# Linear attention's output projection made token-major, with the queries ahead of the values and a third exponential buffer

## What is computed

```
Q, K = phi(h @ Wq), phi(h @ Wk)          # phi(x) = elu(x) + 1; 16 heads of 64
V    = h @ Wv
S, z = cumsum(K (x) V), cumsum(K)        # over the tokens of a sequence
out  = (Q . S) / max(Q . z, 1e-6)        # per head, per token
x    = x + out @ Wo                      # Wo is 1024 x 128: the output projection
```

## Time and profile before

| what | value |
|---|---|
| median of 3 runs | 841.12 us (841.11 to 843.43) |
| profiled execution, its own time | 841.11 us |
| its span | 839.3 us |
| busy: PE, PEld | 790.7 us (94%), 669.6 us (80%) |
| busy: DVE, ACT, POOL | 558.6 us (67%), 571.5 us (68%), 354.2 us (42%) |
| chain that ended last, by engine | PE 68%, ACT 13%, DVE 9%, issue 4%, POOL 4% |
| granted TensorE clock, mean | 0.999 |

### The profile page before, as it was taken

How to read it: one execution, slowest core, us unless ns; L and a number is a source line. 1 busy time by engine, 2 the same in 40 slices (tenths; PEclk the granted TensorE clock), 3 DMA queues, 4 the chain that set the end, 5 groups by cost and what they waited for, 6 DMA issues and landing times.

```text
span 839.3 us, 27765 instructions
## 1 busy us (share of the span) xinstructions
PE 790.7 (94%) x11682; PEld 669.6 (80%) x11682; DVE 558.6 (67%) x1313; ACT 571.5 (68%) x1024; POOL 354.2 (42%) x284
## 2 busy tenths in 40 slices
PE   1799999999999999999999999999889999999997
PEld 0588878877788888888888888888777888888885
DVE  8665656454877877787877867876979682828220
ACT  3787878767646666556666566666578887878774
POOL 4597979774101001010010101000236597979784
PEclk9999999999999999999999999999999999999999
DMA  7001111111000101010010100201015220201010
GB/s 263 0 26 45 57 40 36 35 55 51 16 3 24 29 0 51 0 38 12 0 50 0 51 0 10 78 0 37 28 51 152 76 64 12 63 14 51 1 51 27
DMA packets 56700, 33.53 MB, mean 40 GB/s; under 512 B 1984, under 2 KB 55232, under 8 KB 56640
## 3 DMA queue, kind: packets, MB, share of 16 engines
q1 hardware_dynamic: 56640, 32.79, 13.5%
HBM read 22.29 MB, written 10.49 MB: 39 GB/s over the span
## 4 chain that ended last, share of the span: by engine, by line
PE 68%; ACT 13%; DVE 9%; issue 4%; POOL 4%; DMA 1%; SPq 0%; ACTq 0%; DVEq 0%; POOLq 0%
PE ps L690 33%; PE ps L864 15%; PE ps L661 6%; PE ps L927 4%; PE ps L938 3%; PE ps L758 3%; ACT rr L1236 3%; ACT ee L1235 3%; DVE ol L1662 3%; PE ps L954 2%; ACT vt L1257 2%; ACT kf L1265 2%; PE ps L910 2%; POOL alA L1780 1%; POOL alB L1780 1%
## 5 line engine op out<-in xcount | busy, mean ns | idle before, releaser
L1235 ACT ACTIVATE ee<-ps 128x512 f32<-128x512 f32 x128 | 77.9, 609 | 96.8 <-PE ps L864 62.7
L1880 POOL TENSOR_TENSOR as<-as,power 128x4 f32<-128x4 f32 x16 | 19.0, 1189 | 285.9 <-DVE as L1585 255.7
L1403 DVE SCALAR_TENSOR_TENSOR full<-ps,sc,gate 128x512 f32<-128x512 f32 x64 | 46.6, 748 | 105.8 <-PE ps L690 63.3
L1780 POOL TENSOR_TENSOR alA<-full,ahA 128x512 fp32r<-128x512 f32 x74 | 100.6, 1372 | 35.6 <-DVE ahA L1411 29.5
L690 PE MATMUL ps<-ahA,wh 128*128 128x512 f32 x288 | 113.7, 395 | 1.3 <-POOL alA L1780 1.3
L690 PE MATMUL ps<-ahB,wh 128*128 128x512 f32 x288 | 113.4, 394 | 0.6 <-POOL alB L1780 0.6
L690 PE MATMUL ps<-alA,wh 128*128 128x512 f32 x288 | 112.3, 390 | 0.0
L690 PE MATMUL ps<-alB,wh 128*128 128x512 f32 x288 | 112.2, 390 | 0.0
L1780 POOL TENSOR_TENSOR alB<-full,ahB 128x512 fp32r<-128x512 f32 x76 | 99.5, 1322 | 13.3 <-ACT ahB L1136 7.4
L1135 ACT ACTIVATE full<-ps,sc 128x512 f32<-128x512 f32 x86 | 59.5, 691 | 33.5 <-PE ps L690 23.1
L1236 ACT ACTIVATE rr<-ps 128x512 f32<-128x512 f32 x128 | 78.2, 611 | 0.0
(11 more groups left out here) (181 smaller groups left out, 2178.3 us busy)
## 6 DMA issues: line engine op xcount, KB each, us to landing
wst<-in_ternary SPq DMA_DIRECT2D x5, 512.0 KB, 7.1
stage<-in_attn SPq DMA_DIRECT2D x4, 512.0 KB, 4.8
xlnA<-x_scratch SPq DMA_DIRECT2D x8, 256.0 KB, 2.8
axr<-x_scratch SPq DMA_DIRECT2D x8, 256.0 KB, 3.1
yx_scratch<-ay SPq DMA_DIRECT2D x8, 256.0 KB, 2.3
xs_scratch<-axs SPq DMA_DIRECT2D x8, 256.0 KB, 2.4
xlnA<-yx_scratch SPq DMA_DIRECT2D x8, 256.0 KB, 2.8
xlnB<-yx_scratch SPq DMA_DIRECT2D x8, 256.0 KB, 2.8
```

What stands on the lines that cost most here:

```text
L1235: nc.scalar.activation(ee[k][:, :], src[:, :], ACT.Exp).then_inc(*X["act"].step(f"e_{name}"))
L1403: nc.vector.scalar_tensor_tensor(fulll[m][:, :], ps[f["bank"]["L1", U, m, "v", n]][:, :], sc[:, KT + m:KT + m + 1], gate[k % NS][:, :], AL ...
L1780: return nc.gpsimd.tensor_tensor(dst, src, hi.bitcast(F32), ALU.subtract)
```

## The change

The operands of the output projection change places. The outputs `oh`, `ol` are stationary now, 128 tokens at a time, and Wo moves, 128 columns wide. The result has tokens on the partitions, so the copy to `ayf` and the two transposes go and DVE adds the residual straight from the projection's bank. The query groups are issued before the values on PE, on ACT and in the turns of the banks. A third pair of `ee`, `rr` buffers is added (`NE = 3`). The turn that belonged to the two transposes is still taken, by nothing.

```diff
-            NE = 2
-            ee = [sb(s, f"ee{k}", [P, TILE]) for k in range(NE)]
-            rr = [sb(s, f"rr{k}", [P, TILE]) for k in range(NE)]
+            NE = 3
+            ee = [sb(s, f"ee{k}", [P, TILE]) for k in range(NE - 1)]
+            rr = [sb(s, f"rr{k}", [P, TILE]) for k in range(NE - 1)]
...
-            ayf = sb(s, "ayf", [P, TILE // 2])
...
-            sb(s, "unused4", [P, PR, TILE // 2])
+            ee.append(sb(s, f"ee{NE - 1}", [P, TILE]))
+            rr.append(sb(s, f"rr{NE - 1}", [P, TILE]))
+            sb(s, "unused4", [P, 2, TILE])
...
-                    job(bank, f"WO{hh - 1}", "act", f"wf{hh - 1}")
-                    act.append(f"wf{hh - 1}")
+                    job(bank, f"WO{hh - 1}", "dve", f"y{hh - 1}")
+                    dve.append(f"y{hh - 1}")
...
-                bank = turn()
-                if hh:
-                    job(bank, f"yT{hh - 1}", "dve", f"y{hh - 1}")
-                    dve.append(f"y{hh - 1}")
+                turn()
...
-                for j, h in ((0, None), (1, None), (2, 0), (3, 1)):
+                for j in range(4):
                     phi(turn(), f"Q{hh + 1}.{j}")
-                    if h is not None:
-                        values(turn(), o + 1, h)
+                for h in range(2):
+                    values(turn(), o + 1, h)
...
             def output_projection(hh):
 
                 after("dve", f"ol{2 * hh + 1}.1")
-                three(bank(f"WO{hh}")[:, 0:2 * P],
-                      [(wah[:, 3 * DA + p * P:3 * DA + (p + 1) * P], wal[:, 3 * DA + p * P:3 * DA + (p + 1) * P],
-                        oh[:, p, :], ol[:, p, :]) for p in range(PR)], f"WO{hh}")
+                b = bank(f"WO{hh}")
+                for c in range(2):
+                    own = slice(c * P, (c + 1) * P)
+                    three(b[:, own], [(oh[:, p, own], ol[:, p, own], wah[:, 3 * DA + p * P:3 * DA + (p + 1) * P],
+                                       wal[:, 3 * DA + p * P:3 * DA + (p + 1) * P]) for p in range(PR)], f"WO{hh}" if c else None)
...
-                queries(hh + 1, 0)
-                queries(hh + 1, 1)
-                queries(hh + 1, 2)
-                token_major("V", o + 1, 0)
-                queries(hh + 1, 3)
-                token_major("V", o + 1, 1)
+                for j in range(4):
+                    queries(hh + 1, j)
+                for h in range(2):
+                    token_major("V", o + 1, h)
...
-            def output_rows(hh):
-                after("pe", f"WO{hh}")
...
-                nc.scalar.copy(ayf[:, :], ps[X["banks"].bank[f"WO{hh}"]][:, 0:2 * P]).then_inc(*X["act"].step(f"wf{hh}"))
...
             def residual(hh):
...
-                after("pe", f"yT{hh}")
+                after("pe", f"WO{hh}")
...
-                nc.vector.tensor_tensor(ay[:, own, :], ps[X["banks"].bank[f"yT{hh}"]][:, 0:2 * P].rearrange("p (q d) -> p q d", d=D),
+                nc.vector.tensor_tensor(ay[:, own, :], ps[X["banks"].bank[f"WO{hh}"]][:, 0:2 * P].rearrange("p (q d) -> p q d", d=D),
                                         axp[i % 2][:, own, :], ALU.add).then_inc(*X["dve"].step(f"y{hh}"))
```

More of the change, by code:

```diff
@@ L223, in build_kernel @@
             sb(s, "unused3", [P, 2, D])
-            NE = 2
-            ee = [sb(s, f"ee{k}", [P, TILE]) for k in range(NE)]
-            rr = [sb(s, f"rr{k}", [P, TILE]) for k in range(NE)]
+            NE = 3
+            ee = [sb(s, f"ee{k}", [P, TILE]) for k in range(NE - 1)]
+            rr = [sb(s, f"rr{k}", [P, TILE]) for k in range(NE - 1)]
             kf = sb(s, "kf", [P, PR, P])
             axr = sb(s, "axr", [P, Q, D])
-            ayf = sb(s, "ayf", [P, TILE // 2])
+            sb(s, "unused5", [P, TILE // 2])
             sb(s, "unused2", [P, TILE // 2])
@@ L478, in attention_plan @@
                     tail(1, "W0", "act_fy", "y", 0)
-                    job(2, f"WO{hh}", "act", f"wf{hh}")
-                    act.append(f"wf{hh}")
-                    job(7, f"yT{hh}", "dve", f"y{hh}")
+                    job(2, f"WO{hh}", "dve", f"y{hh}")
                     dve.append(f"y{hh}")
@@ L783, in f_last @@
                 elif t:
-                    after("act", f"wf{NHALF - 1}")
+                    after("dve", f"y{NHALF - 1}")
                 else:
@@ L810, in ffn_pe @@
                         tern_norm(0, "A", NI)
-                    if t == 2:
-                        back(NHALF - 1)
                     f_first(t, range(KT))
@@ L962, in transposed_outputs @@
                     transposes(bank(f"OT{g}.{j}"), [ot[:, 2 * p:2 * p + 2, :] for p in range(4 * j, 4 * j + 4)], X["pe"], f"OT{g}.{j}")
-            def back(hh):
-                after("act", f"wf{hh}")
-                transposes(bank(f"yT{hh}"), [ayf[:, q * P:(q + 1) * P] for q in range(2)], X["pe"], f"yT{hh}")
             def output_projection(hh):
                 after("dve", f"ol{2 * hh + 1}.1")
-                three(bank(f"WO{hh}")[:, 0:2 * P],
-                      [(wah[:, 3 * DA + p * P:3 * DA + (p + 1) * P], wal[:, 3 * DA + p * P:3 * DA + (p + 1) * P],
-                        oh[:, p, :], ol[:, p, :]) for p in range(PR)], f"WO{hh}")
+                b = bank(f"WO{hh}")
[3 more added lines that the diff above has]
+                                       wal[:, 3 * DA + p * P:3 * DA + (p + 1) * P]) for p in range(PR)], f"WO{hh}" if c else None)
             def attention_first():
@@ L999, in pair @@
                 transposed_keys(o)
-                if hh:
-                    back(hh - 1)
                 transposed_outputs(e)
@@ L1277, in outputs_high @@
                         .then_inc(*X["act"].step(f"oh{g}.{j}"))
-            def output_rows(hh):
-                after("pe", f"WO{hh}")
-                if hh:
-                    after("pe", f"yT{hh - 1}")
-                nc.scalar.copy(ayf[:, :], ps[X["banks"].bank[f"WO{hh}"]][:, 0:2 * P]).then_inc(*X["act"].step(f"wf{hh}"))
             def attention_first():
@@ L1308, in attention_act @@
                         f_norm(0)
-                    if hh:
-                        output_rows(hh - 1)
                     transposed_keys(o)
@@ L1320, in attention_act @@
                         f_evacuate(0)
-                        output_rows(hh)
                         continue
@@ L1324, in attention_act @@
                         exp_relu(f"K{o + 1}.{h}")
[L1325 to L1330, removed]
+                    for j in range(4):
+                        exp_relu(f"Q{hh + 1}.{j}")
+                    for h in range(2):
+                        values(o + 1, h)
                     transposed_keys(o + 1)
```

## The result

The changed kernel takes 872.52 us (median of 4 runs, 869.53 to 876.09) against 842.27 us for the kernel before in the same comparison (841.11 to 844.25): a ratio of 1.0357, 95% interval 1.0311 to 1.0404. The forecast was 874 us in a range of 846 to 884, with 0.90 on slower.

What follows compares the result with a forecast made beforehand. The prediction took PE to bound the attention halves. Its sum was 841.11 us + 38.7 for the projection - 6 for the third buffer and query order = 873.8, so 874 us, in a range of 846 to 884.

Steps and rivals of the forecast that it cites:

- The bound: In the attention stage's halves PE sets the time; without `once` a half would take about 27.2 us, with it 27.5.
- The product's price: Each of 48 projection products costs 115 ns by its weight load: 2.42 us more per half, 38.7 us over 16.
- The 81 ns of the Trainium skill: The skill's figure per 128-column matmul in a sustained stream; the projection would take 3.9 us, 0.8 us more per half.
- The copy and the residual: ACT's 16 dropped copies, 6.0 us, were costed at nothing; DVE's residual delays nobody, since `ol` still waits for ACT.
- Queries first, third buffer: PE gets about 0.85 us back in 7 halves with `once`, the order itself winning about 0: -6 us in all.
- The end of the stage: Near the last two projections PE also waits for DVE; up to 1.3 us could vanish there, left to the range.
- the clock: Sign of being wrong: a granted clock under 1.00 in the projection, PE moving columns only half the time.
- Rival 1: In the projection loads are hidden and columns set the price, 65 ns per product: 835.4 us, faster; chance 0.08.
- rival 2: In the projection loads are half hidden, 81 ns per product: 847.7 us; chance 0.05.
- rival 3: In the projection narrow fp32r products cost as plain f32, 244 ns each: 973 us; chance 0.09.
- Rival 4: For the queries, ACT's chain to `ol` stays as long and the -6 us become 0: 880 us; chance 0.10.

Runs made afterwards that it cites:

- e5: Changed kernel with each projection product loading 64 columns of weights instead of 128, same 128 moving columns, half the projection's rows left out: 833.09 us, single run.
- e6: Changed kernel with each projection product moving 64 columns of Wo instead of 128, same load, half the projection's columns left out: 913.63 us, single run.
- e9: e7 with high and low Wo side by side, so 32 products and loads per projection replace 48, and DVE adds twice: 845.88 us, ratio 1.0036.
- e1: Kernel before with the third buffer pair and the queries ahead of the values, old projection kept: 836.56 us, ratio 0.9925.
- e2: Changed kernel with two buffer pairs and the old order, so the new projection alone: 881.32 us, ratio 1.0427 against the kernel before.
- e10: Changed kernel run again unchanged; with its first set, 5 of 9 runs took 875.05 to 878.54 us, the others 869.53 to 870.43.
- e4: Kernel before with only the queries issued ahead of the values, on PE, ACT and in the banks' turns: 842.12 us, ratio 0.9999.
- e3: Kernel before with only the third buffer pair added: 837.68 us, ratio 0.9938.
- e7: Changed kernel with the last half's output projection issued on PE ahead of the transposes that wait for DVE: 869.35 us.
- e8: e1 with the last half's projection issued ahead of the transposes that wait for DVE: 836.08 us, ratio 0.9928 against the kernel before.

## Why the prediction was right, and where it was off

- **The bound.** Right. PE bounded the halves, and 2.21 us more on PE per projection gave 14.74 us first parts in place of 12.48. A half without `once` takes 27.11 us and one with it 27.10, for the 27.2 and 27.5 I had named.
- **The product's price.** I took 115 ns between the load's floor of 110 and the 120 ns of a 256-column product. It is 110.6: the floor itself. The term of the sum mis-sized is 38.7 us, which measured is 35.4, near the lower end I gave (34.9). e5 and e6 show the mechanism, that the load sets it, and e9 that the number of loads does.
- **The 81 ns of the Trainium skill** ("TensorE: Matmul & The Clock Gate", "Back-to-back issue gap"): no run agrees, 110.6 ns for a 128-column fp32r product. It was right not to let it set the sum. The same page of the Trainium skill, in "LDWEIGHTS (loading the stationary operand)", gives the time of a load in ns as its columns divided by 1.2, which is 107 for 128 and 53 for 64. The trace agrees for 128, at 110 ns between starts. For 64 it can't tell: e5's 60 ns may be the load's or that of the 128 moving columns, which I had put at 65 ns from the earlier trace rows.
- **The copy and the residual.** Right at nothing: ACT's idle time before `kf` took the copy's place, and `ol` still waits for ACT's `oh`, 45.5 us in all.
- **Queries first, third buffer.** The -6 us was right as a sum, in part by luck. The second parts of 15 halves add up to 6.1 us less than before, but what this part of the change gives is about 5: 4.9 us in e1 and 5.2 between e2 and the changed kernel, at full clock. In the trace 5.1 us come from six halves with `once`, 0.83 to 0.90 each, the price I had named. The seventh I had counted, the first half, is 0.7 us longer here and 0.15 in e10, and not shorter, and the second half, which I had at nothing, is 1.7 shorter, mostly by idle time of PE that is gone with the new projection (e2). The reading that the order wins nothing was right (e4), and so was the one that ACT's wait for `qf` was the thing to remove (e3). That Q3 would still meet a rest of the wait was right in two of these halves, with second parts of 12.53 and 12.50 us: there Q3 starts 0.70 and 0.66 us after the relu of Q2, where 0.48 is usual. The rest is 0.2 us, too short for a row among the waits.
- **The end of the stage.** There the forecast missed something that it had only named as a sign of being wrong: the clock. At full clock the sum by measured terms is 841.1 + 35.4 - 6.1 = 870.4 us, against 869.53 and 869.99. The other half of the runs lie 5 to 6 us higher with a clock fallen to 1.2 GHz for a while, and so pull the median to 872.52. My 874 came closer to the median than it deserved: a price 3.3 us too high stood in for a loss I had not priced.
- **The rivals.** Rival 1 (65 ns) and rival 2 (81 ns) fall with the measured spacing, rival 3 (244 ns) as well: narrow fp32r products have no price of their own, they wait for loads. Rival 4 falls with e1. The point that decides, which I put at 65 ns under rival 1, was wrong: there the projection alone breaks even. With the 6 us given back it is (3.10 + 6/16) / 48 = 72 ns.

## What to carry to other kernels

Count the weight loads of a product stream and not only its columns: swapping the operands kept 6144 columns and doubled the loads, and the loads became the price. An orientation that saves a copy and a transpose is worth it only if the moving side stays wide enough to hide the load, here 256 columns for a 128-column fp32r load; when it is put in one change with a real gain (the third buffer, some 5 us), measure them apart. And read ACT's idle time first: a copy that leaves an engine which waits for PE anyway saves nothing. Last, a wait that is moved off one instruction can come back at the next that needs the same chain or bank, as in e7 and e8.

## What the hardware showed that I had not expected

The granted clock can fall while PE is busy without a gap. In e6 it went to 0.50 inside a projection, or just behind it, in every half, with 64 columns moved per 110 ns load. In the changed kernel, with 128 columns per load, the looped halves kept 1.00, and it fell where 2.3 us of waiting stood right ahead; it then stayed down for 10.2 us of busy PE (13.7 in e10 and e2), three to four times as long as at the same place in e3 and e5. A stream bound by loads can thus be dearer than its spacing at full clock says: e6's first parts took 16.1 to 18.0 us where 14.7 is what their spacing asks, and the changed kernel's fifteenth projection 3.5 us more than the others. What in the stream brings the clock down stays open: only e6, against the changed kernel, varies the columns under the same load, in one run, and the short falls of e9 and of the first network stand elsewhere than at a stream of such loads.
